# Fourth mixture of experts: the sums of the gated results move from VectorE to GpSimd

## The reference, cut to what matters

```python
E, D, H, O, TOPK = 8, 128, 256, 128, 2
# for all tokens x (already normalised), gate (tokens x 8), zero outside the best two
y = 0
for e in range(E):
    hidden = gelu(x @ W1[e] + b1[e])          # 128 -> 256
    y = y + gate[:, e] * (hidden @ W2[e] + b2[e])   # 256 -> 128
h = h + y
```

## Time and profile before

| | |
|---|---|
| Time, median of 3 runs | 1234.58 us (1231.76 to 1241.58) |
| Profiled execution | 1236.1 us, of which the span from first to last instruction is 1234.3 us |
| Granted TensorE clock, mean over the span | 0.938 |
| Busy over the span | PE 89%, PEld 74%, DVE 73%, ACT 68%, POOL 43% |
| The changed stage | blocks 5 to 39 of f2, 881.8 us to about 972 us from the span's start |

### The profile page before, as it was taken

How to read it: one execution, slowest core, us unless ns; L and a number is a source line. 1 busy time by engine, 2 the same in 40 slices (tenths; PEclk the granted TensorE clock), 3 DMA queues, 4 the chain that set the end, 5 groups by cost and what they waited for, 6 DMA issues and landing times. The chain is left out here.

```text
span 1234.3 us, 29279 instructions
## 1 busy us (share of the span) xinstructions
PE 1098.2 (89%) x8508; PEld 910.6 (74%) x8508; DVE 904.1 (73%) x2770; ACT 845.1 (68%) x2821; POOL 526.2 (43%) x885
## 2 busy tenths in 40 slices
PE   8999979999998999887388599998899899869996
PEld 5778857888887788776288477786678688657884
DVE  0488847999976889956565488886899788755774
ACT  1498858888885555557243378887788499846995
POOL 0379864444304278855252653323342011034552
PEclk9999989999999999988599689999999999959997
DMA  7300002322210000001522200000333100024441
GB/s 293 96 2 3 2 1 63 110 71 65 65 43 23 1 2 1 2 1 38 195 61 50 63 14 2 11 2 2 115 113 113 34 3 2 2 80 122 131 130 36
DMA packets 50824, 66.68 MB, mean 54 GB/s; under 512 B 8100, under 2 KB 30904, under 8 KB 50552
## 3 DMA queue, kind: packets, MB, share of 16 engines
q1 hardware_dynamic: 44552, 53.39, 14.2%
q0 software_dynamic: 4432, 6.59, 2.1%
q10 hardware_dynamic: 1696, 4.98, 1.0%
HBM read 58.32 MB, written 6.71 MB: 53 GB/s over the span
## 5 line engine op out<-in xcount | busy, mean ns | idle before, releaser
L495 DVE TENSOR_TENSOR f_parts<-T,f_parts 128x512 fp32r<-128x512 f32 (+1 forms) x240 | 181.7, 796 | 21.1 <-ACT f_parts L479 19.6
L471 ACT ACTIVATE T<-quad_bank,f_b1s 128x512 f32<-128x512 f32 (+1 forms) x240 | 150.5, 648 | 43.2 <-PE quad_bank L442 34.3
L442 PE MATMUL quad_bank<-XP,f_wp 128*128 128x512 f32 (+1 forms) x720 | 165.3, 373 | 1.1 <-ACT T L471 1.1
L442 PEld LDWEIGHTS quad_bank<-XP,f_wp 128*128 128x128 f32 x720 | 125.6, 188 | 26.4 <-ACT T L471 1.4
L479 ACT ACTIVATE f_parts<-T 128x512 fp32r<-128x512 f32 (+1 forms) x240 | 132.7, 593 | 0.0
L954 ACT ACTIVATE a_late<-quad_bank,a_shift 108x108 f32<-108x108 f32 x352 | 119.1, 363 | 2.7 <-DVE a_shift L1022 2.4
L455 PE MATMUL bank<-f_parts,f_wp 128*128 128x512 f32 (+1 forms) x480 | 116.7, 379 | 4.7 <-DVE XT L504 2.0
L455 PEld LDWEIGHTS bank<-f_parts,f_wp 128*128 128x128 f32 x480 | 85.4, 192 | 23.5 <-DVE a_late L524 2.8
L384 POOL TENSOR_TENSOR f_wp<-f_ws,const 128x512 fp32r<-128x512 f32 (+1 forms) x32 | 31.0, 968 | 122.3 <-DMA f_ws<-in_f_w 53.9
L954 ACT ACTIVATION_READ_ACCUMULATOR a_late<-quad_bank,a_shift 108x1 f32 x352 | 77.2, 219 | 0.0
L765 POOL TENSOR_TENSOR a_ve<-a_mv,const 108x1 f32<-108x1 f32 x44 | 8.3, 189 | 152.1 <-DVE a_mv L1079 152.0
(11 more groups left out here) (470 smaller groups left out, 3105.9 us busy)
## 6 DMA issues: line engine op xcount, KB each, us to landing
a_late<-f_gates SPq DMA_DIRECT2D x64, 256.0 KB, 3.2
a_wqk<-in_a_wqk SPq DMA_DIRECT2D x24, 256.0 KB, 2.5
f_ws<-in_f_w SPq DMA_DIRECT2D x16, 256.0 KB, 3.8
pats<-in_patches SPq DMA_DIRECT2D x5, 648.0 KB, 10.7
pats<-in_patches ACTq DMA_DIRECT2D x5, 648.0 KB, 14.8
a_late<-f_gates SPq DMA_DIRECT2D x16, 128.0 KB, 3.6
f_w1a<-in_f_w SPq DMA_DIRECT2D x1, 2048.0 KB, 11.4
f_w2a<-in_f_w SPq DMA_DIRECT2D x1, 2048.0 KB, 16.2
```

Of the source, the lines that this page charges most:

```text
L442: mm = pe.matmul(self.m.quad_bank[:, q % 4, 0:w], self.wp[0][:, e % 2, a, c * 128:(c + 1) * 128], self.xp[:, b, t0:t0 + w], start=((a, b) ...
L471: act.activation(self.full[:, q % 4, 0:w], self.m.quad_bank[:, q % 4, 0:w], self.func, bias=self.b1s[:, e * self.chunks + c:e * self.chunk ...
L495: dve.tensor_tensor(self.lo[:, q % self.ring, 0:w], self.full[:, q % 4, 0:w], self.hi[:, q % self.ring, 0:w], ALU.subtract).then_inc(self. ...
```

## The change

In f2 alone the 35 additions of `add` are issued by POOL. DVE keeps `lows`, `gated`, `raw` and `finish`. On POOL the adds of expert e - 1 are queued behind both weight splits of expert e; those of expert 1 alternate with the five `lazy` instructions, and those of expert 7 come last. The semaphores and their values stay as they are.

```diff
-    def add(self, dve, i):
+    def add(self, eng, i):
         e, n, t0, w = self.block(i)
-        dve.wait_ge(self.y_used, i + 1)
+        eng.wait_ge(self.y_used, i + 1)
...
-        dve.tensor_tensor(x, x, self.gated_y[:, i % 2, 0:w], ALU.add).then_inc(self.summed, 1)
+        eng.tensor_tensor(x, x, self.gated_y[:, i % 2, 0:w], ALU.add).then_inc(self.summed, 1)
...
             self.split_up(pool, e)
             self.split_down(pool, e)
-            for n in range(self.nb if e == 2 else 0):
-                self.lazy(pool, n)
+            for n in range(self.nb if e > 1 else 0):
+                if e == 2:
+                    self.lazy(pool, n)
+                if self.adds:
+                    self.add(pool, (e - 1) * self.nb + n)
             if self.aside is not None and e > 2:
                 self.aside.piece(pool, e - 3)
+        for n in range(self.nb if self.adds else 0):
+            self.add(pool, (self.experts - 1) * self.nb + n)
...
             self.gated(dve, i)
-            if i > nb and e < self.experts - 1:
+            if not self.adds and i > nb and e < self.experts - 1:
                 self.add(dve, i - 1)
             if e == self.experts - 1:
-                if n == 0:
+                if not self.adds and n == 0:
                     self.add(dve, i - 1)
-                self.add(dve, i)
+                if not self.adds:
+                    self.add(dve, i)
```

More of the change, by code:

```diff
@@ L264, with __init__ @@
 class Mixture:
-    def __init__(self, nc, m, ctx, sem, name, io, bias, func, experts, chunks, gates, room, lead, aside=None):
+    def __init__(self, nc, m, ctx, sem, name, io, bias, func, experts, chunks, gates, room, lead, aside=None, adds=False):
+        self.adds = adds
         self.aside = aside
@@ L525, in gated @@
                                  in1=self.gb[:, k % 4, 0:w], op0=ALU.add, op1=ALU.mult).then_inc(self.y_used, 1)
-    def add(self, dve, i):
+    def add(self, eng, i):
         e, n, t0, w = self.block(i)
-        dve.wait_ge(self.y_used, i + 1)
+        eng.wait_ge(self.y_used, i + 1)
         if e == 1:
-            dve.wait_ge(self.lazied, n + 1)
+            eng.wait_ge(self.lazied, n + 1)
         else:
-            dve.wait_ge(self.summed, i - 2 * self.nb + 1)
+            eng.wait_ge(self.summed, i - 2 * self.nb + 1)
         x = self.sums[:, t0:t0 + w]
-        dve.tensor_tensor(x, x, self.gated_y[:, i % 2, 0:w], ALU.add).then_inc(self.summed, 1)
+        eng.tensor_tensor(x, x, self.gated_y[:, i % 2, 0:w], ALU.add).then_inc(self.summed, 1)
     def logits(self, dve, psum, first, end, part):
@@ L3093, in build @@
             fold = Fold(nc, m, early, io)
-            f2 = lambda nc, m, ctx, sem, room: Mixture(nc, m, ctx, sem, "f2", io, m.small("none", p=128), ACT.Gelu_apprx_tanh, 8, 2, best_gates, room, 2, fold)
+            f2 = lambda nc, m, ctx, sem, room: Mixture(nc, m, ctx, sem, "f2", io, m.small("none", p=128), ACT.Gelu_apprx_tanh, 8, 2, best_gates, room, 2, fold, adds=True)
             with ExitStack() as between:
```

## The result

The changed kernel takes 1247.6 us (median) against 1234.6 us. Two of its 19 executions, of 1561 and 3502 us, were in a slow state and are left out of the ratio, which is 1.0095, 95% interval 1.0077 to 1.0112, or 11.7 us more. The profiled execution has a span of 1242.5 us, but the stages between f0 and f2, whose code is the same in both, took 4.6 us less in it than in the profile of before (497.7 against 502.3 us from the last gate of f0 to gate 5 of f2). Over the profiles of all kernels here this distance goes from 494.5 to 503.5 us where nothing in it was changed, so the profiles are compared within the stage: by the starts of DVE's gates.

The account below looks back on a forecast made before the run. PE was taken to set the pace before the change and DVE after it. Terms of 7.7 + 2.0 - 0.7 gave +9.0 us, from a median of 1234.6 to 1243.6, say 1244, with a range of 1231 to 1253.

Parts of the forecast that it names:

- What bounds it: Main stretch of f2: PE sets the pace at 12.49 us per expert, and DVE follows with no time over.
- Turns at a shared read: DVE instructions with both tensors in SBUF and POOL instructions exclude each other; a low grows 1.11 us, gates are untouched.
- Where the adds fall: Each POOL add goes between DVE's two lows; a large block then takes DVE 2.98 us against PE's 2.77.
- The splits: Weight splits on POOL, now 1.2 us per expert, would cost about 0.6 after the change, bounds 0 and 1.2.
- Gate 12 to gate 37 as a whole: Five experts of f2 would take 69.9 us against 62.25, +7.7 us, bounds +0.2 and +11.3.
- Blocks 5 to 11: Gate 5 to gate 12 of f2 would take 2.0 us more, bounds -2.7 and +2.8.
- The end: From gate 37 on: about 1.2 us come back, last add and hand-overs cost 0.5; together -0.7 us.
- The hidden adds: Rival: adds run under DVE's gates, PE leads again; 1232.6 us at best, about 1234; chance 0.24.
- The wait behind the splits: Rival: adds queued behind both splits on POOL hold DVE's gates and lows; 1254 us; chance 0.07.
- The clock: Rival: PE's granted clock falls to 0.74, an expert takes PE 16.9 us; 1258 us; chance 0.04.

Follow-up runs that it names:

- e1: The changed kernel with each POOL add in f2 replaced by a memset of the same tile, which reads nothing; 1232.1 us, ratio 0.9974.
- e7: The changed kernel with f2's lows reading one tensor from PSUM, adds still on POOL; median 1235.0 us, ratio 0.9997 against the kernel before.
- e13: The changed kernel with f2's lows reading from PSUM and its first transposes one block later, f0 left as it was; 1229.2 us, ratio 0.9964.
- e10: The changed kernel with POOL adding only the first half of each block's columns; 1230.1 us in one run.
- e2: The changed kernel with each POOL add also waiting for both lows of block i + 3, to start beside the next gate; 1245.9 us, ratio 1.0094.
- e6: The changed kernel with split_down placed behind the first add of an expert, from expert 3 on; ratio 1.0082.
- e5: The changed kernel with PE issuing the first transposes of the sums one block later; gate 34 to gate 39 took 10.1 us, 12.7 in the changed kernel.
- e8: Lows reading one tensor from PSUM in f2, with the adds on DVE as in the kernel before; ratio 0.9987.

## Why the prediction was right, and where its sizes were off

**What bounds it.** Right. PE set the pace at 12.5 us per expert, and every version in which DVE's lows are free or the holds are small comes back to that pace (12.51 in e1, e7 and e13, 12.52 in e10).

**Turns at a shared read.** Right, and shown from both sides: take the reads of the adds away from POOL (e1) or one of the two SBUF tensors from DVE (e7) and the adds no longer stretch the lows, in e7 with adds of full length. The period of a large block was forecast as 2.98 us and was 2.97. An add so costs DVE 1.10 us (2.97 against 1.87 without it), not its whole 1.29.

**Where the adds fall.** Right: between the two lows. The rival place, under the gate, was made in e2: 2.61 us per block, 0.36 less.

**The splits.** Under-sized: the sum had 0.6 us per expert. An expert took 14.51 us; less the forecast's 13.53 for one without splits, whose large block (2.97) the profile bears out, that leaves 0.98. Over four experts the difference is 1.5 us. Stepping had put two of the four under gates; the adds that queue behind them then meet both of the small lows (2.99 us for the pair). That e6, with the splits apart, has the same pace speaks for the amount of reading and against the order.

**Gate 12 to gate 37 as a whole**, +10.7 in place of +7.7: 1.5 of the missing 3.0 us are the splits. The rest comes from a wait that the prediction had not priced: its "end" looked only at the last add and the last transposes, and took the first transposes, which PE issues in the middle of the last expert, at nothing. PE stood there for 2.4 us, and its clock was 0.50 for the three microseconds behind. Without that hold the last expert is 2.6 us shorter (e5). Between gates 34 and 37 it took 9.05 us, with the hold but at full clock 7.73 (e6), without the hold 7.54 (e5), so nearly all of the 1.5 us in front of gate 37 is the low clock; the hold itself shows behind gate 37. In the kernel before, PE waited 0.2 us in all for DVE's adds at its transposes, since DVE was not late.

**Blocks 5 to 11**, +1.2 in place of +2.0: between its bounds. **The end**, -0.1 in place of -0.7: gates 37 and 39 came 0.4 us closer, not 1.2, and the hand-over cost 0.3. The hold is why: without it they came 1.5 us closer (2.5 us in e5).

**The rivals.** The hidden adds did not happen, by the order of release. The wait behind the splits did not either: no row has DVE waiting for a POOL add, and e6 has the same pace. It was e2's late adds that brought this wait about. The clock did not fall as the rival had it: it was 1.00 up to block 36, so an expert of PE's work never became the longer one. But it fell to 0.50 for three microseconds in the last expert, which the prediction had at nothing.

The sum was 9.0 us against 11.7 measured. The sign, the mechanism and the place were right; the cost of the splits was too small, and the hold at the first transposes, with the low clock behind it, was left out. Part of the nearness is luck: blocks 5 to 11 came 0.8 us under their term, which hides part of what was missed elsewhere.

## What to carry to other kernels

Before an instruction moves from VectorE to GpSimd, count tensors and not time: if both it and what VectorE does meanwhile read two tensors from SBUF, they ran one after the other here, and most of the GpSimd instruction's length (1.10 of 1.29 us) was added to VectorE's queue. A pair that conflicts can be freed from the other side: here the subtraction read its first operand from PSUM and the stretching was gone. Together with later transposes that made the kernel 0.4% faster than before, where the move alone made it 0.9% slower; what the move adds to that is 0.2 us where it was measured by itself (e7 against e8). The price is a PSUM bank that is held longer, so look at PE's waits in the first blocks too. When an addition gets later, look also at who waits for it in a queue in order (the transposes), not only at the last one, and at the clock of PE behind such a wait.

## What the runs showed that was not expected

A low with one tensor in PSUM is no slower than one with both in SBUF: 0.681 us in e7 against 0.680 before (medians of the records), though a gate of the same width takes 0.74. ACT writing the gelu back into its own bank took 0.67 us for 512 columns (0.69 before, into SBUF), and reading the copy from PSUM 0.60 (0.63).

DVE was full over the whole stage, but in e1 its relief was worth something only at both ends: with the adds gone from DVE and no reads on POOL, blocks 5 to 11 fell from 20.5 to 17.0 us, and the last expert from 11.0 to 9.7, while the main stretch stayed at 55.8 (55.2 before).
